# Cross-attention mask of the row maxima moved from TensorE to VectorE, normalisations moved to GpSimd, every engine's order rewritten and unrolled, contexts, masks and outputs moved four batches at a time

## The reference

```python
x = x + _L0_attn_ref(_layernorm(x), ...)          # self-attention "S", with a relative position bias
x = x + _L0_xattn_ref(_layernorm(x), ctx_1024, ctx_1024, mask, ...)   # cross-attention "X"
x = x + _L0_ffn_ref(_layernorm(x), ...)           # feed-forward "F"

# in the cross-attention
scores = jnp.einsum('bhqd,bhkd->bhqk', q, k) * scale
scores = jnp.where(mask[:, None, :, :] == 0, jnp.float32(NEG_INF), scores)
attn = jax.nn.softmax(scores, axis=-1)
# in the feed-forward: ternary weights, activations rounded to 8 bits by row
xq = jnp.clip(jnp.round(x * scale), -128.0, 127.0) / scale
```

## Time and profile before

| | us |
|---|---|
| median of 3 runs | 514.36 |
| lowest and highest | 513.71, 518.05 |
| span of the profiled execution | 513.4 |
| PE busy | 454.1 |
| DVE busy | 398.0 |
| ACT busy | 372.9 |
| POOL busy | 254.6 |

### The profile page before, as it was taken

The page is one execution under the profiler, slowest core; times in us unless marked ns, Lnnn a source line. Parts: engine busy times, 40 slices in busy tenths (PEclk is TensorE's granted clock), DMA queues, the critical chain, the costliest instruction groups (busy, mean ns, idle before and its releaser), DMA issues.

```text
span 513.4 us, 18365 instructions
## 1 busy us (share of the span) xinstructions
PE 454.1 (88%) x5596; PEld 328.0 (64%) x5596; DVE 398.0 (78%) x1154; ACT 372.9 (73%) x993; POOL 254.6 (50%) x691
## 2 busy tenths in 40 slices
PE   2246889999999999999999999999999999997762
PEld 1224556777777777777777777777777777764440
DVE  5722446799888889888888988889888888877553
ACT  0222556788888888888888888888888887775451
POOL 4221445655565555555566655555556654434110
PEclk9999789999999999999999999999999999999785
DMA  6264255555455545454445555544454555223000
GB/s 186 77 192 107 72 143 142 140 142 141 134 134 144 141 122 145 139 135 131 122 138 135 135 128 135 137 135 122 133 137 137 137 137 136 79 86 92 23 7 10
DMA packets 82191, 62.48 MB, mean 122 GB/s; under 512 B 57634, under 2 KB 71714, under 8 KB 82146
## 3 DMA queue, kind: packets, MB, share of 16 engines
q1 hardware_dynamic: 82146, 61.92, 44.4%
HBM read 46.47 MB, written 14.88 MB: 119 GB/s over the span
## 4 chain that ended last, share of the span: by engine, by line
PE 78%; DVE 5%; DMA 4%; issue 4%; SPq 3%; ACT 3%; POOL 1%; DVEq 0%; POOLq 0%; ACTq 0%
PE bank L1117 14%; PE bank L1092 12%; PE bank L1059 11%; PE bank L1088 6%; PE bank L1055 6%; PE bank L1264 4%; PE bank L1210 3%; PE bank L1138 2%; PE bank L1237 2%; PE bank L1175 2%; PE bank L1154 2%; PE bank L1295 2%; PE bank L1303 2%; PE bank L1224 2%; PE bank L1196 2%
## 5 line engine op out<-in xcount | busy, mean ns | idle before, releaser
L533 ACT ACTIVATE probs<-bank 128x512 f32<-128x512 f32 x256 | 145.5, 597 | 32.0 <-PE bank L1092 31.7
L826 DVE TENSOR_REDUCE neg_max_S<-bank 128x4 f32<-128x512 f32 x128 | 87.1, 685 | 34.3 <-PE bank L1059 34.2
L826 DVE TENSOR_REDUCE neg_max_X<-bank 128x4 f32<-128x512 f32 x128 | 84.2, 676 | 8.9 <-PE bank L1059 5.7
L1059 PE MATMUL bank<-stack_k_S,stack_q_S 120*128 120x128 bf16 x512 | 46.9, 227 | 12.9 <-DMA stack_k_S<-scratch_S 12.4
L432 POOL TENSOR_TENSOR qk_rest_X<-qk_X,qk_parts_X 128x256 f32<-128x256 f32 x32 | 21.4, 670 | 70.8 <-ACT qk_parts_X L536 70.8
L1092 PE MATMUL bank<-stack_q_S,stack_k_S 122*128 122x128 bf16 x512 | 52.5, 229 | 4.5 <-DMA stack_q_S<-neg_maxT_S 4.5
L1117 PE MATMUL bank<-probs,v_aug_S 128*32 128x128 f32 x1024 | 55.5, 291 | 0.0
L1055 PE MATMUL bank<-mask_bias,ident_bf 128*128 128x512 bf16 x128 | 49.4, 386 | 3.6 <-issue 2.3
L1092 PEld LDWEIGHTS bank<-stack_q_X,stack_k_X 74*128 74x128 bf16 x512 | 40.6, 99 | 16.4 <-issue 1.6
L1092 PE MATMUL bank<-stack_q_X,stack_k_X 74*128 74x128 bf16 x512 | 50.8, 222 | 0.0
L1088 PE MATMUL bank<-ident_bf,mask_bias 128*128 128x512 bf16 x128 | 50.3, 393 | 0.0
(11 more groups left out here) (159 smaller groups left out, 1159.1 us busy)
## 6 DMA issues: line engine op xcount, KB each, us to landing
stack_q_S<-scratch_S SPq DMA_DIRECT2D x32, 288.0 KB
stack_k_S<-scratch_S SPq DMA_DIRECT2D x96, 96.0 KB
stack_q_X<-scratch_X SPq DMA_DIRECT2D x32, 288.0 KB
stack_k_X<-scratch_X SPq DMA_DIRECT2D x96, 96.0 KB
scratch_S<-qk_parts_S SPq DMA_DIRECT2D x32, 192.0 KB, 2.3
scratch_X<-qk_parts_X SPq DMA_DIRECT2D x32, 192.0 KB, 2.3
ctx_in<-ctx SPq DMA_DIRECT2D x32, 64.0 KB, 2.7
mask_in<-mask SPq DMA_DIRECT2D x32, 64.0 KB, 1.8
```

The source lines that it names most:

```text
L533: act.activation(probs[:, c, :], bank_b[c % 2][:, :], ACT.Exp).then_inc(sems["exp_" + a], 1)
L826: dve.tensor_reduce(neg_max[a][:, first_head(c):first_head(c) + 2 * HC - 1:2], bank_a[c % 2][:, :].rearrange("i (h j) -> i h j", h=HC), AX ...
L1059: last = pe.matmul(bank[:, part_of_bank(hh)], stack_q[a][rows, p, head(c, hh)], stack_k[a][rows, p, head(c, hh)], start=not masked, stop=n ...
```

## The change

- **Mask of the maxima.** `scores_a` no longer writes the mask bias for X (`BIASED = (0, 1, 2, 3)` names all chunks). VectorE does it in `row_max`: in place of one reduction of 512 columns, four `tensor_tensor_reduce` of 128 columns, each adding the mask bias to a head's scores, negating, and keeping the minimum. `scores_b` keeps its mask matmul.
- **Normalisations.** `normalise` (S, X, F) and `quantise_y` are GpSimd's now, and GpSimd also negates the mean (`negate_mean`).
- **Data.** The context comes already transposed, so its transpose on TensorE and copy on ScalarE go. All 32 contexts and masks have a place of their own; SP loads them in groups of four (256 KB each) without a wait, and stores four batches at a time except for the last four.
- **Buffers.** `probs` and `o_raw` one for S and one for X, four copies of `v_aug`; v is projected together with q and k; `xnT` of X leaves from the output's bank.
- **Maxima transposed** as 128 columns rather than 32.
- **Orders.** The loop is gone: 43 steps, from -1 to 41, are unrolled on every engine, and the order of the work within a step is new on all of them. The waits for a shared PSUM bank are listed by hand behind each TensorE operation.

```diff
-LOOP_FROM, LOOP_TO = 10, 30
+STEPS = [(t, t) for t in range(-1, B + 10)]
+V_COPIES = 4
+GROUP, GROUP_LAG = 4, 2
-WARM = 4
+WARM, WARM_BATCHES = 4, 4
+BIASED = (0, 1, 2, 3)
...
-        ctx_in = sb("ctx_in", [S, 2, D])
-        mask_in = sb("mask_in", [S, 2, S], I32)
-        ctxT = sb("ctxT", [D, 2, S])
+        mask_in = sb("mask_in", [S, B, S], I32)
+        ctxT = sb("ctxT", [D, B, S])
-        probs = sb("probs", [S, CH, HC * S])
-        o_raw = sb("o_raw", [128, 2, S])
+        probs = {a: sb(f"probs_{a}", [S, CH, HC * S]) for a in "SX"}
+        o_raw = {a: sb(f"o_raw_{a}", [128, 2, S]) for a in "SX"}
+        neg_mean = {k: sb(f"neg_mean_{k}", [S, 1]) for k in "SXF"}
+        biased = sb("biased", [S, CH, HC, S], BF16)
...
+            def group_load(st):
+                n = st.of("X", GROUP_LAG)
+                if n is None or n % GROUP:
+                    return
+                batches = slice(n, n + GROUP)
+                sp.dma_start(ctxT[:, batches, :], ctx[batches].rearrange("b d s -> d b s"))\
+                    .then_inc(sems[f"ctx_loaded{n // GROUP % 2}"], 16)
+                sp.dma_start(mask_in[:, batches, :], mask[batches].rearrange("b s t -> s b t"))\
+                    .then_inc(sems[f"mask_loaded{n // GROUP % 2}"], 16)
...
+            # SyncE's step
+                group_load(st)
+                store(st, 10)
+                parts_out("S", st, 0)
+                stack_in("X", st, 4)
+                max_in("X", st, 5)
+                stack_in("S", st, 0)
+                parts_out("X", st, 3)
+                max_in("S", st, 1)
...
+            # GpSimd
+            def normalise(k, st, lag):
+                pool.tensor_scalar(xn[k][:], x_all[:, b, :], neg_mean[k][:, 0:1], rstd[k][:, 0:1],
+                                   ALU.add, ALU.mult).then_inc(sems["xn_" + k], 1)
...
+            # VectorE, row_max
+                if a == "X" and c in BIASED:
+                    for hh in range(HC):
+                        head = first_head(c) + 2 * hh
+                        last = dve.tensor_tensor_reduce(biased[:, c, hh, :], quarter(bank_a[c % 2], hh), mask_bias[:, b % 2, :],
+                                                        -1.0, -2.0 * BIG, ALU.add, ALU.min,
+                                                        neg_max[a][:, head:head + 1])
+                    last.then_inc(sems["max_" + a], 1)
...
+            # TensorE, scores_a
+                masked = a == "X" and c not in BIASED
```

More of the change, by code:

```diff
@@ new lines, in add_shift, with rest @@
+            def add_shift(a, st, lag):
+                b = st.of(a, lag)
+                if b is None or (a == "S" and b == 0 and st is not START):
+                    return
+                pool.wait_ge(sems["xn_" + a], done(b))
+                pool.tensor_tensor(x_all[:, b, :], x_all[:, b, :], shift[a][:], ALU.add)\
+                    .then_inc(sems["shifted_" + a], 1)
+            def rest(a, st, lag):
+                b = st.of(a, lag)
+                if b is None:
+                    return
+                pool.wait_ge(sems["part1_" + a], done(b))
+                if b:
+                    pool.wait_ge(sems["part3_" + a], done(b - 1))
@@ L554, in xnT_out @@
[L554 to L566 removed]
+                act.wait_ge(sems["av_" + a], done(b, CH))
@@ L577, in qk_out @@
-            def qk_out(a, st, b):
-                if not b:
-                    return
-                act.wait_ge(sems["qk_ps_" + a], b.count())
-                if a == "S" and st.seq(V_S):
-                    act.wait_ge(sems["v_ps_S"], st.seq(V_S).count())
-                if b.before(1):
-                    act.wait_ge(sems["rest_" + a], b.before(1).count())
-                for m, name in enumerate(("q_", "k_")):
-                    act.activation(qk[a][:, m, :], quarter(bank_p, m), ACT.Identity,
-                                   bias=qk_bias[a][:, m:m + 1]).then_inc(sems[name + a], 1)
@@ L995, in _ @@
+                h_inverse(st, 8)
+                row_max("S", st, 2, 1)
+            run(step)
         @block.tensor
@@ new lines, in scores_a @@
+                if masked:
+                    pe.wait_ge(sems["mask_bias"], done(b))
+                    pe.matmul(bank[:, :], ident_bf[:], mask_bias[:, b % 2, :].unsqueeze(1).to_broadcast([S, HC, S]),
+                              start=True, stop=False)
+                for hh in range(HC):
+                    last = pe.matmul(bank[:, part_of_bank(hh)], stack_q[a][rows, b % 2, head(c, hh)],
+                                     stack_k[a][rows, b % 2, head(c, hh)], start=not masked,
+                                     stop=not masked or hh == HC - 1)
@@ new lines, in scores_a, with scores_b @@
+                last.then_inc(sems["score_a_" + a], 1)
+            def scores_b(a, st, lag, c, *users):
+                b = st.of(a, lag)
+                if b is None:
+                    return
+                bank, rows = bank_b[c % 2], slice(0, A_ROWS[a] + M_ROWS)
+                after(pe, st, *users)
+                if c == 0 and a == "S" and b < WARM_BATCHES:
+                    keep_warm(bank)
+                if c == 0:
+                    pe.wait_ge(sems[f"max_in_{a}{b % 2}"], loaded(b, 16))
@@ L1094, in scores_b, with attend @@
+                    last = pe.matmul(bank[:, part_of_bank(hh)], stack_k[a][rows, b % 2, head(c, hh)],
+                                     stack_q[a][rows, b % 2, head(c, hh)], start=not masked,
                                      stop=not masked or hh == HC - 1)
                 last.then_inc(sems["score_b_" + a], 1)
-            def attend(a, st, b, c):
-                if not b:
+            def attend(a, st, lag, c, *users):
+                b = st.of(a, lag)
+                if b is None:
```

1259 lines of the change are left out of this document (569 added, 690 removed).

## The result

The changed kernel takes 493.99 us (median of 4 runs, 492.23 to 499.67) where the kernel before, beside it, takes 516.2 (4 runs, 513.71 to 520.06): a ratio of 0.9555 with a 95% interval of 0.9493 to 0.9616. Beside the experiments it was run once more, as `a_control`: 496.74 us, ratio 0.9629, interval 0.9564 to 0.9695. The forecast was 497 us in 480 to 522, so it holds; several of its terms do not, and they happened to cancel. Ratios are taken over fast executions alone, which leaves out one of 496.22 us in `a_load_1` and the 499.67 here. That one was profiled (span 497.8), so where steps are compared the profile of `a_control` (span 493.2) stands beside it.

What follows compares the result with a forecast made beforehand. PE looked full but hid slack, with DVE as near to being the bound. DVE's 11.7 us plus 0.8 of waits made steps of 12.5, not 13.33: 23 steps -19 us, fill +1.5, giving 497 us, range 480 to 522.

Steps and rivals of the forecast that it cites:

- c: VectorE: time from one new tensor_tensor_reduce to the next, taken as 0.235 us, sixteen a step, 3.8 us.
- The rule of the DRAIN: VectorE: next operation starts only once the pipeline has emptied; would make c 0.29 and the step 0.9 us longer; not followed.
- The first rival: VectorE: the new operation is dear, c at 0.36 us, DVE occupied 13.7 us a step, 543 us in all; chance 0.16.
- VectorE's sum: VectorE's occupation a step: 12.1 us less 1.55 and 2.7, plus 3.8 for the new operations, giving 11.7 us.
- The waits: VectorE: of 1.16 us of waits a step, 0.35 go and 0.81 stay, making the step 12.5 us.
- The third rival: PE and ACT are the next bound, DVE is not: c 0.20, step 11.8 us, 480 us; chance 0.16.
- TensorE: TensorE's step: four mask matmuls and the context's transpose go, worth 1.0 us, leaving 12.3 if PE alone set it.
- The loop: Hardware loop's turns go: 0.5 us x 5, taken as already inside the 13.33 us step; unrolled code shows no stall.
- GpSimd: GpSimd gets three normalisations and y_q, 1.8 to 2.6 us, plus means 0.6; busy 10.3 to 11.1 us a step.
- The second rival: GpSimd, in order, returns about one us of waits a step: no gain in steps, 513 to 516 us; chance 0.16.
- Fill and drain: Start and end of the kernel: fill +1.5 us (bounds 0 and 3) for the larger early loads; drain left unchanged.
- the fifth rival: TensorE's granted clock falls with more gaps: five per cent, 0.6 us a step, still covered by DVE; no chance of its own.

Runs made afterwards that it cites:

- a_load_1: Changed kernel with contexts and masks loaded one batch at a time, every step, in place of groups of four: 492.09 us, ratio 0.9475.
- a_mask_pe: Changed kernel with the mask of the maxima put back on TensorE, all else kept: 510.2 us, ratio 0.9891 to the kernel before.
- b_both: Kernel before, unrolled, old orders and buffers, with the maxima's mask on VectorE and normalisations, negated means and y_q on GpSimd: 644.23 us, ratio 1.247.
- a_x_early: Changed kernel with the last 24 batches of x and every group of contexts and masks issued one step earlier: 495.83 us, ratio 0.9585.

## Why the prediction was right, and where it was not

**The new operation: right, c a little lower.** Groups of DVE in after (busy us, mean ns, idle before), and its timeline:

```profile
L824 DVE CUSTOM_DVE_ANT_0 biased<-bank,mask_bias 128x128 bf16<-128x128 f32 x512 | 113.0, 286 | 17.2 <-PE bank L1049 17.0
...
L824 DVE DVE_READ_ACCUMULATOR2_ANT neg_max_X<- 128x1 f32 x512 | 42.4, 83 | 0.0
```

```profile
262.32 0.28 DVE L824 CUSTOM_DVE_ANT_0 biased<-bank,mask_bias 128x128 bf16<-128x128 f32 x1
262.53 0.08 DVE L824 DVE_READ_ACCUMULATOR2_ANT neg_max_X<- 128x1 f32 x1
262.53 0.28 DVE L824 CUSTOM_DVE_ANT_0 biased<-bank,mask_bias 128x128 bf16<-128x128 f32 x1
262.74 0.08 DVE L824 DVE_READ_ACCUMULATOR2_ANT neg_max_X<- 128x1 f32 x1
```

c is 262.53 - 262.32 = 0.21 us; the prediction took 0.235, the middle of 0.20 and 0.27. It is two instructions, as the Trainium skill says in "VectorE: DVE Perf Modes", section "Two Vector instructions with no wait between them", but the second lies inside the next one's time and adds at most 0.01. The rule of the DRAIN, weighed in the prediction, would have made c at least 0.28. The prediction gave only half of it: the same section of the Trainium skill, "The DRAIN you can't avoid", adds that a next operation that is not held starts earlier. The 0.21 us between operations of 0.28 agree with that; they do not stand against the page. The first rival, 543 us, falls with this.

**VectorE's sum: right.** 7.9 + 16 x 0.21 = 11.3 us, measured 11.46 busy in a step of 11.79. Without the new operations and with the four reductions it should be 7.9 + 2.7 = 10.6; `a_mask_pe` has 10.69.

**The waits: right in size, of another kind.** The prediction carried 0.8 us of waits over from the earlier trace rows and got 11.7 + 0.8 = 12.5. Over the 23 steps DVE is busy 11.46 us a step and idle 0.68 in `a_control`, 11.47 and 0.87 in after. So most of the difference to 12.14 and 12.34 is the occupation, put 0.24 us too high, for the most part by c (16 x 0.025 = 0.4). But the 0.8 us were taken as waits of every step, and an undisturbed one has 0.33; the rest comes irregularly, as PE's waits for late X stacks and DVE's behind it. The mean of `a_control` lies below the forecast's range of steps, 12.2 to 12.9, that of after at its lower edge. The third rival named this case (a step of 11.8 with DVE not the bound); the step was right and its reason half right, since DVE and PE bound it together. Its 480 us were not reached because of the fill, the drain and the disturbances.

**TensorE: wrong.** It was put at 12.3 us a step from 13.3 less 1.0. `a_mask_pe` has all of its old matmuls but the context's transpose and fits into 12.42, and without the mask PE is busy for 11.59. The 40.00 of 40 in the earlier trace rows hid about 0.8 us a step. The prediction said that this share hides slack and then used it as the base of its sum all the same.

**The loop: wrong.** It was put at nothing beyond what the 13.33 holds, because the unrolled steps of the earlier trace rows took 13.18. Unrolled throughout, the old kernel has steps of 13.01 and gains 2.4%. The rows were read in the wrong place: batch 21's tanh at 383.45 stands in step 29, still in the loop. The first two steps of the same trace are unrolled and have every stage at work:

```profile
103.27 0.71 ACT L656 ACTIVATE tanh_g<-bank,gate_half 128x512 f32<-128x512 f32 x1
...
116.30 0.71 ACT L656 ACTIVATE tanh_g<-bank,gate_half 128x512 f32<-128x512 f32 x1
...
129.39 0.69 ACT L656 ACTIVATE tanh_g<-bank,gate_half 128x512 f32<-128x512 f32 x1
```

They take 13.03 and 13.09 us. And the turns' ends are four, not five, 2.0 us in all.

**GpSimd: right in size; that its order cost nothing was assumed, not worked out.** The groups of POOL in after:

```profile
L406 POOL TENSOR_SCALAR xn_X<-x_all,neg_mean_X,rstd_X 128x128 f32<-128x128 f32 x32 | 14.3, 447 | 5.5 <-issue 5.3 <-POOL rstd_X L394 0.2
...
L416 POOL TENSOR_SCALAR y_q<-xn_F,y_inv 128x128 f16<-128x128 f32 x32 | 11.8, 367 | 25.8 <-DVE y_inv L887 25.4
...
L384 POOL TENSOR_SCALAR neg_mean_F<-mv_F 128x1 f32<-128x1 f32 x32 | 7.6, 238 | 2.5
```

Three normalisations at 0.447 and `y_q` at 0.367 are 1.71 us, just under the lower bound of 1.8; with the means POOL is busy 10.0 us a step (forecast 10.3 to 11.1). `y_q` waits 0.8 us a batch for `y_inv`, harmlessly. DVE does not wait for `xn` or `y_q`, which the prediction named as a sign of being wrong. `b_both` shows what the same four operations cost in the old order: over 4 us a step. The second rival had the mechanism (GpSimd, in order, hands its results over late) and put it at one microsecond; it doesn't occur in the new order.

**Fill and drain: too small.** The fill was put at +1.5 us for the 512 KB group. It is +3.4 to +4.8 and comes from the place of the loads in SP's queue, behind the maxima of batch 0 and ahead of the parts of batch 2, and hardly from the group's size (which is also 0.38 MB more than before, not 0.45: a context and a mask were 128 KB). `a_x_early` gets all of it back. The drain was left unchanged and became 2.3 to 3.8 us longer, in `a_control` mostly by the clock: the fifth rival was looked at for the steady part alone, where the clock is 1.00 as it said. In a late window it is 0.79 where it was 0.95.

The sum in its own terms: 23 steps -19 (measured -22.7 in after, -27.3 in `a_control`), fill +1.5 (+4.8, +3.4), drain 0 (+2.3, +3.8). The total of -17.5 against -15.6 and -20.2 is right because a term that was too cautious met two that were too small. That is luck, as it is that the loop, put at nothing, and TensorE, put 0.7 us a step too high, did not move the sum, which went by VectorE.

## What to carry to other kernels

When work moves between engines, sum the occupation of every engine first, from start-to-start distances; a part that overloads its new engine alone (here the mask, 2.3% slower) can still pay once another part has made room. Then redo the in-order lists: the same placement took 18.2 us a step in the old orders and 11.8 in the rebuilt kernel, so the order is as much a part of the change as the placement. Look at fill and drain by themselves: bulk loads belong into a stretch of the queue where it would wait anyway, and where TensorE half idles, a few matmuls with no use keep its clock up.

## What was unexpected of the hardware

- Unrolling a hardware loop of four long steps was worth 2.4% of the time: 0.5 us at each turn's end, 0.25 us in each step inside, and a remainder in the fill and the drain whose cause is open.
- An operation with an accumulated result shows as two instructions, 286 and 83 ns, but follows its like after 0.21 us.
- On GpSimd `xn_X` (f32 out, both operands a column) takes 447 ns and `y_q` (f16 out, one operand a column and one a constant) 367, both 128x128 from f32. Which of the two differences does it was not tried.
- TensorE's granted clock went from 1.00 to 0.50 right behind 3 us in which it was busy for 1.4, twice in one execution; with the clock kept up the two steps were 1.8 and 2.9 us shorter, and the steps ahead of them 0.8 us longer each.
